# A graph network kernel: the edge-weight matrix summed with swapped operands and kept as float32, and four more blocks a pass taken by matrix products

## What is computed

```python
x = x + attention(h, src, dst)                          # 4 heads, softmax over a node's edges
x = x + max_pool_layer(max_pool_layer(h))               # m = relu(h @ Wp + bp); segment_max(m[src], dst)
support = h @ weight_G
x = x + segment_sum(support[src] * edge_weight, dst) + bias_G
x = x + propagate(h, 16 steps)                          # h = 0.9 * segment_sum(norm * h[row], col) + 0.1 * x
```

## Time and profile before

| | |
|---|---|
| median of 3 runs | 2656.03 us (2645.49 to 2656.1) |
| profiled execution | 2653.48 us, of which the span of its instructions is 2651.7 us |
| PE busy | 2444.7 us (92%) |
| DVE busy | 1827.7 us (69%) |
| ACT busy | 1252.1 us (47%) |
| POOL busy | 1110.2 us (42%) |

### The profile page before, as it was taken

The page is one execution under the profiler, slowest core; times in us unless marked ns, Lnnn a source line. Parts: engine busy times, 40 slices in busy tenths (PEclk is TensorE's granted clock), DMA queues, the critical chain, the costliest instruction groups (busy, mean ns, idle before and its releaser), DMA issues. The chain is left out here.

```text
span 2651.7 us, 72943 instructions
## 1 busy us (share of the span) xinstructions
PE 2444.7 (92%) x29368; PEld 1998.7 (75%) x29368; DVE 1827.7 (69%) x5033; ACT 1252.1 (47%) x2985; POOL 1110.2 (42%) x1375
## 2 busy tenths in 40 slices
PE   6998999996899999579999984698999999999999
PEld 4666777775677777456777763597999999999998
DVE  6997999996899999359999982302444444444444
ACT  4997888886666666346666652202211111111110
POOL 4105999993777777557777764200000000000000
PEclk7557999996999999689999995599999999999999
DMA  5103000003466666536666665295000000000000
GB/s 174 44 2 105 13 12 13 12 12 112 119 162 160 159 157 152 148 81 157 157 154 158 160 187 140 92 344 196 2 2 2 2 2 2 2 2 2 2 2 20
DMA packets 147302, 226.90 MB, mean 86 GB/s; under 512 B 55184, under 2 KB 113259, under 8 KB 146290
## 3 DMA queue, kind: packets, MB, share of 16 engines
q1 hardware_dynamic: 121502, 185.74, 23.4%
q0 software_dynamic: 21920, 35.15, 6.7%
q10 hardware_dynamic: 3540, 1.30, 0.2%
HBM read 121.74 MB, written 100.35 MB: 84 GB/s over the span
## 5 line engine op out<-in xcount | busy, mean ns | idle before, releaser
L1886 POOL DMA_INDIRECT max_row<-table,max_src_rows x608 | 646.1, 1063 | 279.6 <-issue 146.6
L1920 PE MATMUL max_far<-adj 128*96 128x512 f16 x2200 | 560.0, 382 | 4.0 <-DVE adj L2041 4.0
L1758 POOL TENSOR_SCALAR e<-e 128x512 f32<-128x512 f32 (+1 forms) x625 | 365.9, 604 | 178.6 <-ACT e L1746 161.3
L2404 PE MATMUL prop<-g,adj 128*128 128x192 f16 x4608 | 386.9, 247 | 8.8 <-DVE g L2478 8.8
L1772 DVE TENSOR_TENSOR e<-e,a_ps 128x1024 f32<-128x1024 f32 (+1 forms) x313 | 372.4, 1195 | 32.9 <-PE a_ps L1684 12.9
L2404 PEld LDWEIGHTS prop<-g,adj 128*128 128x128 f16 x4608 | 380.4, 98 | 13.7 <-issue 9.2
L2404 PE MATMUL prop<-weights_then_states,adj 128*128 128x192 f16 x4608 | 384.3, 246 | 0.0
L2404 PEld LDWEIGHTS prop<-weights_then_states,adj 128*128 128x128 f16 x4608 | 378.9, 98 | 3.7 <-issue 2.5
L1746 ACT ACTIVATE e<-s_ps 128x512 f32<-128x512 f32 (+1 forms) x625 | 335.6, 585 | 60.4 <-PE o_ps L1696 36.2
L2041 DVE TENSOR_SCALAR adj<-adj,node_numbers 128x512 f16<-128x512 f16 x1100 | 350.5, 343 | 13.7 <-PE max_far L1920 7.0
L1920 PEld LDWEIGHTS max_far<-adj 128*96 128x96 f16 x2200 | 252.8, 128 | 120.6 <-DVE adj L2041 6.9
(11 more groups left out here) (287 smaller groups left out, 3577.8 us busy)
## 6 DMA issues: line engine op xcount, KB each, us to landing
weights_then_states<-weights SPq DMA_DIRECT2D x100, 400.0 KB, 5.0
weights<-max_rows_w SPq DMA_DIRECT2D x52, 400.0 KB
rows_dram<-max_out SPq DMA_DIRECT2D x100, 192.0 KB, 2.1
weights<-adj SPq DMA_DIRECT2D x48, 400.0 KB
max_same<-same_dram SPq DMA_DIRECT2D x196, 96.0 KB, 3.2
rows_dram<-adj SPq DMA_DIRECT2D x96, 192.0 KB, 5.7
max_row<-table,max_src_rows POOLq DMA_INDIRECT x608
adj<-ids_dram SPq DMA_DIRECT2D x44, 128.0 KB, 3.7
```

The source lines that it names most:

```text
L1758: nc.gpsimd.tensor_scalar(e_tile(u), e_tile(u), math.exp(10.0), math.exp(-10.0), ALU.min, ALU.max).then_inc(clipped, 1)
L1886: nc.gpsimd.indirect_dma_start(row[i % RING][:, j, :], None, table_dram, bass.IndirectOffsetOnAxis(ap=src_rows[:, 4 * n + j:4 * n + j + 1] ...
L1920: mm = nc.tensor.matmul(far_ps[j % 2][0:D, :], parts[:, k, a, :], hot[(T * j + k) % HOTS], start=k == a == 0, stop=k == T - 1 and a == 1)
L2404: return nc.tensor.matmul(sums(step, t), adj[:, k, t * P:(t + 1) * P], states[:, k, :], start=start and t % 2 == 0, stop=k == END - 1 and ...
```

## The change

- lay_out swaps its operands: the keys (125 columns) are stationary, the 128 lanes move, and PSUM holds (destination in window, source tile) on 125 partitions and the source lane in 128 columns for each window. Three PSUM banks instead of two and a bank for pieces.
- high_part, low_part, turn_piece and keep_piece go. ACT copies a step's strip as float32 (keep_strip), and SP stores each step's strip in one DMA, every fourth in two, in rows of 512 bytes. Four strip buffers. weights_dram becomes (T, 2, 64, NP) float32, of the same size in bytes.
- support is kept as float32 by one ACT copy (keep_support); keep_low of the third layer goes.
- The weighted sum reads W as 125 pieces of 128 x 640 float32 into seven slots, and multiplies each 128 x 128 tile once with the float32 support: 625 products. The five banks are finished one after the other by the last five loads.
- FAR has 26 blocks instead of 22: 4, 8, 12, 15, 19, 23, 26 and so on to 96, that is 4, 4 and 3 apart.

```diff
-FAR = range(4, 92, 4)
+FAR = [11 * (j // 3) + 4 * (j % 3 + 1) for j in range(26)]
...
-            def keep_high(g):
+            def keep_support(g):
                 m = DENSE[g][1]
                 act.wait_ge(multiplied, g + 1)
-                nc.scalar.activation(parts[:, tiles(g), 0, :], out_ps[g % 2][:, 0:m * D].rearrange("p (t d) -> p t d", d=D), ACT.Copy, scale=ROW_SCALE).then_inc(hi_kept, 1)
+                nc.scalar.activation(support[:, tiles(g), :], out_ps[g % 2][:, 0:m * D].rearrange("p (t d) -> p t d", d=D), ACT.Copy).then_inc(support_kept, 1)
...
-        strip = sb("strip", [P, 2, T, 2, HALF], F16)
-        strip_ps = [ps(f"strip_ps{i}") for i in range(2)]
-        piece_ps = ctx.enter_context(nc.psum_tensor(f"{name}_piece", [P, 1024], F16))
+        STRIPS = 4
+        strip = [sb(f"strip{i}", [FEW_KEYS, WIDEST, P], F32) for i in range(STRIPS)]
+        strip_ps = [ps(f"strip_ps{i}") for i in range(3)]
...
             def lay_out(n):
-                if n >= 2:
-
-                    pe.wait_ge(lo_kept, n - 1)
+                if n >= 3:
+
+                    pe.wait_ge(strip_kept, n - 2)
...
                     for h in range(2):
-                        mm = nc.tensor.matmul(by_source(n)[:, :, FEW * w:FEW * w + m], lanes_by_weight(n)[:, h, w, :], keys_of,
-                                              start=w == 0 and h == 0, stop=h == 1, skip_group_check=True)
+                        mm = nc.tensor.matmul(strip_ps[n % 3][0:FEW_KEYS, w * P:(w + 1) * P], key_hot[n % 2][:, w, 0:FEW_KEYS], lanes_by_weight(n)[:, h, w, :],
+                                              start=h == 0, stop=h == 1, skip_group_check=True)
                 mm.then_inc(hots_used, 1)
...
-                for i, q in pieces_of(m):
-                    turn_piece(i, q)
...
-                if 1 <= m <= PARTS:
-                    low_part(m - 1)
...
+            def keep_strip(n):
                 act.wait_ge(hots_used, n + 1)
+                if n >= STRIPS:
+
+                    act.wait_ge(strip_stored[n % STRIPS], stored_until(n - STRIPS))
+                nc.scalar.activation(strip[n % STRIPS][:, 0:STEP_WINS[n % QUARTER], :].rearrange("r w p -> r (w p)"), strip_sums(n), ACT.Copy).then_inc(strip_kept, 1)
...
+            def store_strip(n):
+                sp.wait_ge(strip_kept, n + 1)
+                whole = STEP_DST[n % QUARTER] // FEW
+                sp.dma_start(strip_rows(n)[0:FEW_KEYS * whole, :].rearrange("(w r) p -> r w p", r=FEW_KEYS), strip[n % STRIPS][:, 0:whole, :]).then_inc(strip_stored[n % STRIPS], 16)
+                if stores_of(n) == 2:
+                    left = T * (STEP_DST[n % QUARTER] - FEW * whole)
+                    sp.dma_start(strip_rows(n)[FEW_KEYS * whole:, :], strip[n % STRIPS][0:left, whole, :]).then_inc(strip_stored[n % STRIPS], 16)
...
-                if m % QUARTER == QUARTER - 1 and QUARTER <= m < PARTS:
-                    store_tile(m // QUARTER - 1)
+                if 1 <= m <= PARTS:
+                    store_strip(m - 1)
...
-    SLOTS, COLUMNS = 6, NP // 2
+    SLOTS, COLUMNS = 7, FIVE * P
...
-        units = [(k, h, s) for k in range(T) for h in range(2) for s in range(2)]
+        units = [(k, b) for k in range(T) for b in range(WEIGHED)]
...
+            for u, (k, b) in enumerate(units):
                 pe.wait_ge(loaded[u % SLOTS], 16 * (u // SLOTS + 1))
...
+                for i in range(FIVE):
+                    mm = nc.tensor.matmul(weighted(FIVE * b + i), w[u % SLOTS][:, i * P:(i + 1) * P], support[:, k, :],
+                                          start=k == 0 and i == 0, stop=k == T - 1, skip_group_check=True)
+                mm.then_inc(used, 1)
...
-                dve.wait_ge(weighed, b + 1)
+                dve.wait_ge(used, len(units) - WEIGHED + b + 1)
...
-            act.wait_ge(weighed, WEIGHED)
+            act.wait_ge(used, len(units))
...
-    weights_dram = scratch("weights", (T, 2, 2, HALF, NP), F16)
+    weights_dram = scratch("weights", (T, 2, HALF, NP))
```

More of the change, by code:

```diff
@@ L779, in scale_up @@
                 nc.vector.scalar_tensor_tensor(shift[:, tiles(g)], mean_var[:, tiles(g), 0], -1.0, scale[:, tiles(g)], ALU.mult, ALU.mult).then_inc(shifted, 1)
[L781 to L785, removed]
             nc.vector.memset(eps[:, :], 1e-5).then_inc(eps_made, 1)
-            for s in range(G + 2):
+            for s in range(G + 1):
                 if s < G:
@@ L1803, in max_pass @@
     WIDEST = max(STEP_WINS)
-    assert RING == QUARTER and sum(PIECES) == T and NB <= PARTS <= P
+    assert RING == QUARTER and NB <= PARTS <= P and WIDEST * P <= 512
     with stack() as ctx:
@@ L1829, in max_pass @@
         keys, lanes, weights = pass_tables(tables)
-        columns = key_order(adj)
+        columns = c.iota16[:, 0:FEW_KEYS]
         behind_out = more[:, T * P + 2 * 8 * D:2 * NP - P]
@@ L1862, in far_tiles, with strip_rows @@
             return []
[L1864 to L1875, removed]
+        strip_sums = lambda n: strip_ps[n % 3][0:FEW_KEYS, 0:STEP_WINS[n % QUARTER] * P]
+        def strip_rows(n):
+            i, q = divmod(n, QUARTER)
+            rows = weights_dram[i, part, :, :].rearrange("d (k p) -> (d k) p", k=T)
+            return rows[T * DST_AT[q]:T * (DST_AT[q] + STEP_DST[q]), :]
+        stores_of = lambda n: 2 if STEP_DST[n % QUARTER] < FEW * STEP_WINS[n % QUARTER] else 1
+        stored_until = lambda n: 16 * sum(stores_of(k) for k in range(n % STRIPS, n + 1, STRIPS))
         assert NB + BACK >= PARTS + 2
@@ L2329, in sum_and_propagate @@
         sem = lambda n: ctx.enter_context(nc.semaphore(n))
-        late = sb("weights_then_states", [P, SLOTS, COLUMNS], F16)
-        w = [late[:, i, :] for i in range(SLOTS)]
-        after = late[:, :, :].rearrange("p s n -> p (s n)")
+        after = sb("weights_then_states", [P, 4 * T * D], F16)
+        w = [after[:, 2 * COLUMNS * i:2 * COLUMNS * (i + 1)].bitcast(F32) for i in range(SLOTS)]
         base = after[:, 0:2 * T * D].bitcast(F32).rearrange("p (t d) -> p t d", d=D)
         g1 = after[:, 2 * T * D:4 * T * D].rearrange("p (t a d) -> p t a d", t=T, a=2)
-        assert SLOTS * COLUMNS >= 4 * T * D and COLUMNS % P == P // 2
+        assert 2 * SLOTS * COLUMNS <= 4 * T * D
         idle = parts[:, :, :, :].rearrange("p t a d -> p (t a d)").bitcast(F32)
@@ L2376, in _ @@
         def _(pe):
-            for u, (k, h, s) in enumerate(units):
+            for u, (k, b) in enumerate(units):
                 pe.wait_ge(loaded[u % SLOTS], 16 * (u // SLOTS + 1))
-                first, last = k == h == 0, k == T - 1 and h == 1
-                for t in range(COLUMNS * s // P, -(-COLUMNS * (s + 1) // P)):
-                    begin, end = max(t * P, COLUMNS * s), min((t + 1) * P, COLUMNS * (s + 1))
-                    rows = slice(begin - t * P, end - t * P)
-                    for r in range(2):
-                        mm = nc.tensor.matmul(weighted(t)[rows, :], w[u % SLOTS][:, begin - COLUMNS * s:end - COLUMNS * s], parts[:, k, r, :],
-                                              start=first and r == 0 and t % FIVE == 0, stop=last and r == 1, skip_group_check=True)
-                    if last and t % FIVE == FIVE - 1:
-                        mm.then_inc(weighed, 1)
-                if u < len(units) - 1:
-                    mm.then_inc(used, 1)
+                for i in range(FIVE):
+                    mm = nc.tensor.matmul(weighted(FIVE * b + i), w[u % SLOTS][:, i * P:(i + 1) * P], support[:, k, :],
+                                          start=k == 0 and i == 0, stop=k == T - 1, skip_group_check=True)
+                mm.then_inc(used, 1)
             pe.wait_ge(looped, T)
```

74 lines of the change are left out of this document (20 added, 54 removed).

## The result

The changed kernel takes 2616.76 us (median of 4 runs, 2613.67 to 2620.99) where the kernel before takes 2653.57: a ratio of 0.987, 95% interval 0.9852 to 0.9888. The forecast was 2628 us, and -28.4 on the profiled execution; its span went from 2651.7 to 2619.2, -32.5.

| stage | before, us | after, us | difference | forecast |
|---|---|---|---|---|
| up to the first gather | 664.4 | 664.3 | -0.1 | 0 |
| first max pass | 449.4 | 421.2 | -28.2 | -25.5 |
| second layer | 57.0 | 58.8 | +1.8 | 0 |
| second max pass | 451.9 | 431.8 | -20.1 | -21.7 |
| third layer | 79.2 | 77.8 | -1.4 | -0.3 |

What follows compares the result with a forecast made beforehand. PE was taken to bound the max passes and float32 records the weighted sum: -25.5 - 21.7 + 19.1 - 0.3 = -28.4 us on 2653.48 gives 2625, forecast 2628 from the runs' median; 8 in 10 range 2609 to 2658.

Steps and rivals of the forecast that it cites:

- The end of the far load: Max passes, PE: the far products' stretch, from m = 9 to 100 instead of 92, ends 15.5 us later, before unevenness.
- The term for unevenness: Max passes: 1%, 4 us a pass, added for uneven steps (25 tiles in three steps, then in four).
- What is late next: Max passes: PE is last at 4.14 us a step, DVE at 4.05 and POOL's gathers at 3.99, each gather 1.37.
- The ends of the passes: After the far load: pass 1 needs 4.5 + 4.3 us instead of 53.8; pass 2 waits 12.2 for the away load.
- Stores at no cost: Max passes: 125 store issues instead of 50, 512-byte packets some 29 ns each; DMA share stays about 0.63.
- The weighted sum: Weighted sum on PE: 625 float32 products, 1250 records at 0.112 us, end 21.8 us later; +19.1 with the early bank.
- The early bank: Weighted sum's end: bank 0 finishes four loads ahead, so the DVE and ACT chain behind it starts 2.7 us earlier.
- Second and third layer: Layers around the second max pass: second unchanged at 0, third -0.3 us for losing its last low part.
- cheap float32: Rival, 8%: the weighted sum stays bound by its loads at its present length; whole 2606 us.
- the gathers undo the passes' gain: Rival, 13%: gathers bound the max passes; from 1.52 us each the whole is 13 us slower, at 1.55 2685 us.
- PE's rival: Rival, 16%: PE bound, with lay_out at 0.068 to 0.073 and records at 0.122 us; 2654, up to 2660 us.
- records did overlap: Answers a 3% rival: the weighted sum's float32 records don't overlap, each taking 0.275 us; whole 2832 us.

## Why the prediction was right, and where it was off

- **The end of the far load** came 18.7 us later (1060.12 to 1078.79), forecast 15.5 + 4. That is partly luck, since three errors cancel. turn_back was costed at its old 0.50 and takes 0.442; lay_out was costed at 0.056 and takes 0.058. With those, 270.8 + 92 x 0.442 + 30.2 + 598 x 0.058 = 376.4 us, 4.1 below the 380.5 of the sum. But the mean step was 4.204 and 4.215 us (84 steps from scan to scan), 92 of them 387 to 388: 10 to 11 us a pass beyond the products, most of it waits for gathers (7.7 and 10.2 in 360 us), where I allowed 4. And the kernel before had such waits too: its 84 steps took 4.386 and 4.369 us each, 368.4 and 367.0 where the sum had 365.0 "with nothing left over", so 2 to 3 us of them are no difference. The term for unevenness was mis-sized on both sides, and turn_back was missed: I took its duration over though the instruction before it changed.
- **What is late next** (PE at 4.14 a step, DVE and POOL 2 to 4% behind): PE's place held, POOL's distance did not. A gather was costed at 1.37 us and comes every 1.39 at best and every 1.42 in the change: 32 of them in eleven steps are 4.04 to 4.13 us a step, against PE's 376.4/92 = 4.09. POOL is level with PE, and the two trade waits, as the kernel with lay_out last shows. The 1.37 was the mean gather of the whole trace and a pause read in the idle end of the pass; it put at nothing POOL's waits for its own gathers to land (26.5 us of 360, 0.10 a gather).
- **The ends of the passes**: in the first 6.8 us from the last far product to the next stage (forecast 8.8); in the second the away load landed last as foreseen, and the next stage began 10.9 us behind its issue (forecast 12.6).
- **Stores at no cost**: right. A 512-byte packet took 28 ns in the mean (13597 of them from 840 to 980; estimate 29), and the DMA share stayed at 0.63.
- **The weighted sum**: two records a product and 0.112 us each were right. 135.1 to 150.7 is 3.5 us less than forecast: the clock rose to 1.0 9.7 us after the first load, not 13, so 37 records were done in the first 11 us and not 32 in 13. The early bank is worth 2.6 us (forecast 2.7): PE's last record ends at about 1800.7, and the propagation's first product starts at 1804.64, 4.0 us behind it (6.5 before).
- **Second and third layer**, +1.8 and -1.4: the second took 56.3 to 59.8 us in all kernels, and the third 76.4 to 78.6 with the change's code and 77.4 to 79.2 with the code before, so this is scatter.
- **The rivals**: cheap float32 would have left the stage at the length of its loads (122.6 us, as the kernel with two of five products shows), and it took 150.7. By the sum the gathers undo the passes' gain only from 1.52 us on, and they came every 1.42. The two prices that PE's rival put at their upper ends were 0.058 and 0.112; records did overlap, 0.112 apart and not 0.275.

## What to carry to other kernels

Cost an operation on a full PE with its neighbour: turn_back's four float32 products took 0.44 us behind a 512-column product and 0.50 behind a 128-column one, as if the first weight load hid behind the longer product. Where two engines are within some per cent of each other, price the change on both; here each half of the change was worth little or a loss without the other, and 5 us more work on PE cost nothing. A float32 product with 128 x 128 weights cost 0.222 us at the full clock with 48 moving columns as with 96, against 2 x 2 x 0.0456 = 0.182 for the four float16 products that it replaced, so it pays only where it takes more off another full engine or stage.

## What the runs showed of the hardware that I had not expected

The clock: 48 moving columns instead of 96, with PE never idle, went with a granted clock of 0.50 instead of 1.00 for 235 us, and the clock rose again behind the return to 96. It is one run. There, fewer columns moved cost 114 us and saved nothing.

The chips: on two of the four chips with a known number, the kernel before takes 2824 and 2785 us instead of 2653. It was not profiled there, but eight other kernels were, and in them all of the difference lies in the two max passes (488 to 523 us each); the second and third layer are within 3 us of the others, and so is the weighted sum where it was left as it is. The stretch 840 to 980 us of the change with 22 blocks, on one of those chips and then on a usual one:

```profile
840.00:980.00 140.00, 113.06 (x728) 73.26 (x727) 101.18 (x267) 49.02 (x127) 79.31 (x78) 0.90 0.46 123
```

```profile
840.00:980.00 140.00, 133.02 (x986) 94.90 (x984) 133.39 (x358) 66.90 (x170) 106.06 (x102) 1.00 0.62 164
```

and what its engines waited for there on the first of them:

```profile
ACT max_strip L2048 <- remote: 40.3, 7, 6.9
POOL max_row L1877 <- PE max_col L1900: 31.4, 5, 7.2
```

Every engine does less, and waits end with updates that the profile can't assign ("remote"). ACT copies a strip at 912.91 us whose products PE began at 906.13 and ended, as modelled, at 906.76: 6 us later. The 512-byte packets are as fast as elsewhere (28 ns in the mean on both chips). What holds PE there was not found. Ratios from such a chip were of use only beside a second run elsewhere: the four blocks alone read 0.997 there and 1.009 on a usual chip.
